# Order of GpSimd's and VectorE's work in a two-layer hypergraph block: the older group's power and the whole xb come first

## What is computed

```
H   = (adj != 0)
D   = 1 / sum_e H[c,e] w[e]          w = first row of adj
B   = 1 / sum_c H[c,e]
conv(x, W, b) = D * H (B * H^T (x W^T)) + b
h   = relu(conv(x, W1, b1))          256 -> 512
h   = layer_norm(h) * gamma + beta
y   = conv(h, W2, b2)                512 -> 256
out = layer_norm(x + (y + x))
```

## Time and profile before

| | |
|---|---|
| time of three executions | 327.19 us median, 326.97 to 327.41 |
| the profiled execution | 326.02 us, its span 324.1 us |
| granted TensorE clock over the span | 0.994 of full speed |
| busy: PE, DVE, ACT, POOL | 291.9, 228.6, 209.5, 143.0 us |
| make_h (L584) and add_pair (L650), 158.18 us, with POOL idle, in the turn shown | 0.42 and 0.68 us |
| one turn of the main loop in mid kernel | 18.98 us (normalise, L478, of two groups running: 132.19 and 151.17 us) |

### The profile page before, as it was taken

One profiled execution on the slowest core, in us unless ns is written; L12 is line 12 of the kernel. 1 busy time (PEld: TensorE's weight loads), 2 busy tenths in 40 slices (PEclk: granted clock), 3 DMA queues, 4 the chain that ended last, 5 costly groups with the idle time before them and its releaser, 6 DMA issues.

```text
span 324.1 us, 5911 instructions
## 1 busy us (share of the span) xinstructions
PE 291.9 (90%) x1866; PEld 251.0 (77%) x1866; DVE 228.6 (71%) x647; ACT 209.5 (65%) x621; POOL 143.0 (44%) x193
## 2 busy tenths in 40 slices
PE   6799889898989989898998989899898989999891
PEld 5689779696877969697795969779596877969690
DVE  2878597676849667685966768597676858668585
ACT  4478675777656577665657866566786656474713
POOL 2243524527064452716445171544617155553723
PEclk9999999999999999999999999999999999999997
DMA  7911400504123050412306042220403301010103
GB/s 237 270 34 50 115 0 14 166 2 141 40 73 107 5 174 3 134 46 59 119 3 179 2 124 54 53 97 3 147 0 115 98 1 67 0 65 2 65 3 129
DMA packets 33511, 24.28 MB, mean 75 GB/s; under 512 B 7932, under 2 KB 33224, under 8 KB 33480
## 3 DMA queue, kind: packets, MB, share of 16 engines
q1 hardware_dynamic: 33376, 23.86, 24.5%
q10 hardware_dynamic: 104, 0.04, 0.0%
HBM read 13.80 MB, written 8.39 MB: 68 GB/s over the span
## 4 chain that ended last, share of the span: by engine, by line
issue 50%; POOL 29%; PE 9%; DVE 8%; ACT 3%; DVEq 0%; POOLq 0%; ACTq 0%
POOL r_hi L858 11%; POOL rstd L842 6%; POOL rstd L865 5%; POOL xb_sb L850 4%; DVE g_sb L636 3%; PE bank_v L274 2%; DVE mv_sb L689 1%; PE bank_s L238 1%; PE bank_v L259 1%; PE bank_s L341 1%; POOL shift L873 1%; PE bank_g L291 1%; DVE var L693 1%; PE bank_g L284 1%; ACT r_sb L466 1%
## 5 line engine op out<-in xcount | busy, mean ns | idle before, releaser
L842 POOL TENSOR_TENSOR rstd<-stat,half_power 128x2 f32<-128x2 f32 x32 | 22.7, 711 | 130.0 <-DVE stat L626 130.0
L858 POOL TENSOR_SCALAR r_hi<-r_sb 128x512 fp32r<-128x512 f32 x64 | 53.0, 836 | 32.2 <-ACT r_sb L466 32.2
L284 PE MATMUL bank_g<-w_hi,r_hi 128*128 128x258 f32 x256 | 65.5, 288 | 0.0
L636 DVE SCALAR_TENSOR_TENSOR g_sb<-bank_g,rstd,c 128x256 f32<-128x256 f32 x64 | 28.1, 480 | 52.5 <-POOL rstd L842 52.5
L478 ACT ACTIVATE z_sb<-z_sb,shift,rstd 128x256 f32<-128x256 f32 x60 | 32.5, 590 | 49.6 <-POOL shift L873 49.6
L286 PE MATMUL bank_g<-w_lo,r_hi 128*128 128x256 f32 x256 | 63.8, 282 | 0.0
L274 PE MATMUL bank_v<-u_hi,w_hi 128*128 128x512 f32 x128 | 52.1, 407 | 10.8 <-ACT r_sb L466 10.2
L274 PE MATMUL bank_v<-u_hi,w_lo 128*128 128x512 f32 x128 | 50.8, 397 | 0.0
L274 PE MATMUL bank_v<-u_lo,w_hi 128*128 128x512 f32 x128 | 50.6, 395 | 0.0
L284 PEld LDWEIGHTS bank_g<-w_hi,r_hi 128*128 128x128 f32 x256 | 48.3, 189 | 1.4
L286 PEld LDWEIGHTS bank_g<-w_lo,r_hi 128*128 128x128 f32 x256 | 48.2, 188 | 1.2
(11 more groups left out here) (98 smaller groups left out, 476.4 us busy)
## 6 DMA issues: line engine op xcount, KB each, us to landing
x_sb<-in_x_dram SPq DMA_DIRECT2D x16, 512.0 KB, 3.9
out_dram<-z_sb SPq DMA_DIRECT2D x15, 512.0 KB, 3.2
adj_sb<-in_adj_dram SPq DMA_DIRECT2D x16, 256.0 KB, 3.7
w_raw<-in_L_gnn_W_dram SPq DMA_DIRECT2D x2, 512.0 KB, 4.9
out_dram<-z_sb SPq DMA_DIRECT2D x2, 256.0 KB, 2.6
turned_h<-h_sb SPq DMA_TRANSPOSE x13, 2.4
b_half<-in_L_gnn_b_dram SPq DMA_DIRECT2D x1, 128.0 KB, 8.1
edge_rows<-in_adj_dram ACTq DMA_DIRECT2D x1, 32.0 KB, 3.2
```

The lines of the kernel that those rows point to most:

```text
L284: pe.matmul(bank_g[:, n, 0:W2COLS], r_hi[:, i % 2, k, graph(n)], w2_hi[:, k], start=(k == 0), stop=False)
L636: ins = nc.vector.scalar_tensor_tensor(out=g_sb[:, n], in0=bank_g[:, n, 0:DOUT], scalar=rstd1[:, n:n + 1], in1=c2[:, :], op0=ALU.mult, op1 ...
L842: nc.gpsimd.tensor_tensor(rstd1[:, part], stat1[:, 3, part], half_power[:, part], ALU.pow).then_inc(rstd1_ready, 1)
L858: nc.gpsimd.tensor_scalar(r_hi[:, i % 2, k], r_sb[:, k], 1.0, 1.0, ALU.mult, ALU.mult).then_inc(r_hi_ready, 1)
```

## The change

On POOL the order of a turn becomes copy_w(i+3), add_b2(i+1) for the whole group, inverse_std2(i-1), inverse_std1(i,0), split_r(i+1,0), split_r(i+1,1), inverse_std1(i,1), split_r(i+1,2), split_r(i+1,3). `add_b2` is one instruction of 128x1024 instead of two of 128x512, and waits for all low parts of the group before (`r_lo_ready`), so that it starts when DVE has done `split_r(i,3)`, beside `split_u`. On DVE `make_var2(i-1)` and `make_h(i+4)` come ahead of `read_g(i,0)`: make_var2 before make_var1(i,0), make_h after it. The counts of `xb_ready` are halved where they are waited for.

```diff
@@ SyncE, load_x
-                    sp.wait_ge(xb_ready, (j - 2) * 2)
+                    sp.wait_ge(xb_ready, j - 2)
@@ PE, ahead of the last group's z
-            pe.wait_ge(xb_ready, G * 2)
+            pe.wait_ge(xb_ready, G)
@@ DVE, make_z
-                    dve.wait_ge(xb_ready, (i + 1) * 2)
+                    dve.wait_ge(xb_ready, i + 1)
@@ DVE, main loop
-                make_var1(i, 0)
-                read_g(i, 0)
                 if i:
                     make_var2(i - 1)
-                    if i + 4 < G:
-                        make_h(i + 4)
+                make_var1(i, 0)
+                if i and i + 4 < G:
+                    make_h(i + 4)
+                read_g(i, 0)
                 split_r(i + 1, 0)
                 make_var1(i, 1)
@@ POOL
-            def add_b2(i, half):
-                part, n = graphs(half), len(each(half))
+            def add_b2(i):
                 pool.wait_ge(x_in[i % 3], landed(i, 3))
-                if i >= 2 and half != 1:
+                if i >= 2:
                     pool.wait_ge(z_ready, (i - 1) * 2)
-                nc.gpsimd.tensor_tensor(xb_sb[:, i % 2, part], x_sb[:, i % 3, part],
-                                        b2_half[:, :].unsqueeze(1).to_broadcast([P, n, DOUT]),
-                                        ALU.add).then_inc(xb_ready, 1 if half is not None else 2)
+                if i:
+                    pool.wait_ge(r_lo_ready, i * KH)
+                nc.gpsimd.tensor_tensor(xb_sb[:, i % 2], x_sb[:, i % 3],
+                                        b2_half[:, :].unsqueeze(1).to_broadcast([P, PER, DOUT]),
+                                        ALU.add).then_inc(xb_ready, 1)
@@ POOL, main loop
-            add_b2(0, None)
+            add_b2(0)
 
             for i in range(LAST):
                 if i + 3 < G:
                     copy_w(i + 3)
-                inverse_std1(i, 0)
-                add_b2(i + 1, 0)
-                split_r(i + 1, 0)
+                add_b2(i + 1)
                 if i:
                     inverse_std2(i - 1)
+                inverse_std1(i, 0)
+                split_r(i + 1, 0)
                 split_r(i + 1, 1)
                 inverse_std1(i, 1)
-                add_b2(i + 1, 1)
                 split_r(i + 1, 2)
                 split_r(i + 1, 3)
```

## The result

The changed kernel takes 299.12 us (median of 4, 298.84 to 299.20) against 327.15 us: a ratio of 0.914, 95% interval 0.9125 to 0.9157. Beside the later experiments it took 299.2 us once more. The forecast was 303.4, in a range of 299.0 to 311.0: the measured time is inside, but only 0.12 us above the low end. The sum's 23.8 us compare with 27.2 us between the two profiled spans.

A forecast was written before the change was run, and what follows sets the result against it. PE, busy 291.9 of 324.1 us, bounds the kernel; its idle time comes from ACT's wait for POOL's late shift. 12 x 1.85 + 2.8 - 1.2 = 23.8 us gained gives a median of 303.4 us, range 299.0 to 311.0.

The forecast's parts named there:

- the low end: Fast bound of the time: 12 turns at 2.2 us plus 3 less 0.5 gives 298.3, taken as 299.0 us.
- The sum: Whole kernel: 12 turns x 1.85, plus 2 x 1.4, less 1.2 us, makes 23.8 us gained.
- What bounds, and the release of ACT: POOL's late shift holds ACT's normalise and ReLUs, delaying PE's make_v chunk 3 and make_y; at most 2.2 us a turn.
- The second half's chain: POOL and DVE from inverse_std1(i,1) to make_z: make_u starts 2.0 us sooner, DVE 0.3 behind PE's best.
- xb beside u_lo: Whole xb on POOL holds DVE's binv (L601) for 0.15 to 0.5 us; 0.15 taken, turn's gain rounded to 1.85.
- The first rival: POOL's split_r(i+1,3) gets the ports before DVE's add_pair: 1.35 us gained a turn, time 309.6 us; chance 0.24.
- The first turn: xb(1) right behind xb(0) holds DVE's two add_pair, u_lo and turn_q: 1.2 us lost, bounds 0 and 2.2.
- The last two turns: Same waits with less ACT work ahead: three quarters of a turn's gain, 1.4 us each, bounds 0.5 and 2.0.

The follow-up runs named there:

- The powers alone: Kernel before with the new order of powers on POOL and make_var2 on DVE, xb still in halves at its old places: 316.4 us, ratio 0.968.
- xb alone: Changed kernel's whole, early xb, with the powers and DVE's order as in the kernel before: 317.9 us, ratio 0.972.
- xb in halves: Changed kernel with xb as two half instructions at the new place: 299.27 us, ratio 0.915.
- half a pad: Changed kernel with one added 128x512 POOL instruction, like half of xb, ahead of xb in turns 1 to 13: 313.9 us, ratio 0.958.
- `make_s` first: Changed kernel with make_s(i+3) ahead of make_u(i+2) on PE: 294.81 us, ratio 0.901.
- The added wait: Changed kernel with xb of group 1 waiting on POOL until add_pairs of group 0 is done: 297.49 us, ratio 0.911.
- an explicit wait: Tested by removing xb's wait for DVE's low parts (`r_lo_ready`) from the changed kernel: 318.8 and 321.3 us, ratio 0.979.
- One program: Changed kernel with a second whole xb-like POOL instruction ahead of xb, turns 1 to 13: 303.65, 324.33, then 302.73, 303.58, 322.52 and 325.07 us.

## Why the prediction was right, and where its sizes were off

*What bounds, and the release of ACT: right.* The wait of L274 is gone, `make_y` took 1.89 us (forecast "about 1.9"). The powers alone and xb alone each give about a third of a turn's gain, so the two parts had to be worked out as one chain on POOL, as they were.

*The second half's chain: right.* I had `make_u` 2.0 us earlier with DVE 0.3 us behind PE's best. It is 2.01 us earlier in each turn; DVE waits 0.28 us for the first half of y at 145.04, and `make_s` in its place gave 0.35 us a turn.

*xb beside u_lo: mis-sized.* I took 0.15 us a turn for xb's hold on binv, 1.8 us in all. xb took 2.40 us, not 2.6 to 2.9 (the 2.88 of the earlier trace rows held a wait for DVE's r_lo ahead of it, as I read it now; that was not tried alone), and ended at 151.60 when binv came: 0.17 us, no hold. (With the 2.88 it would have ended 6.2 us after `make_u`'s start, not 6.25.) Nor would 0.15 have cost anything: in the run with xb in halves a hold of 0.34 us left its turn as long as before. One of 1.0 us cost 0.93 us in the run with half a pad. In the run with `make_s` first 0.5 us cost nothing, but there `make_s` gives cover that the changed kernel lacks, so what 0.5 us costs in the changed kernel no run shows. The rule of the shared ports, taken from the Trainium skill, page "SBUF — State Buffer", section "Who interferes with whom", spoke against the change only if something that matters waits behind xb. Nothing did, and one long xb was no worse than two short ones (299.2 and 299.27 us).

*The first rival: not taken.* DVE did get the ports first: add_pair (144.09) runs 0.68 us and r_hi behind it is held (0.84 at 144.40). r_lo (0.80 us at 143.37) was held as forecast. The rival's order, POOL first, is what happens in the run with half a pad, where add_pair takes 1.10 us and PE waits 0.92 us. DVE was ahead by 0.3 us here, where I had 0.15: the margin was real but small.

*The first turn: mechanism right, size off.* DVE's two add_pair and PE's wait behind them, with PE's later wait for the ReLU:

```profile
27.30 3.32 DVE L650 TENSOR_TENSOR pair_sb<-sq_sb 128x512 f32<-128x512 f32 x2
```

```profile
31.40 0.66 PE L301 MATMUL bank_g<-ident,q_sb 128*128 128x128 f32 x4 [1.31 <-DVE q_sb L657]
...
41.84 2.34 PE L308 MATMUL bank_v<-g_sb,at_sb 128*128 128x256 f32 x8 [1.24 <-ACT r_sb L466]
```

3.32 us instead of 1.26, and 1.31 us of idle PE at turn_q. But the wait at `make_y` fell from 2.4 to 1.24 us, since the half xb that stood ahead of r_hi in that turn is gone too. I had put down 1.2 us; the traces show 0.25 lost, or 0.56 without the earlier start of that execution. The added wait took back 1.7, more than was lost, because it keeps the gain of the missing half xb.

*The last two turns:* 1.3 and 1.6 us against 1.4 each, and 0.5 behind them that I had not counted. The three terms together (1.8, 0.95, 0.65) are the 3.4 us between the sum and the traces; 0.3 of the 0.95 is the earlier start. The median is 4.3 us below the forecast. The other 0.9 us is no part of the mechanism: I had added 1.2 us for a profiled execution below its median, and after the change that distance was 0.28 us. All these errors went the same way, and the time stayed in the range by only 0.12 us. I had worked out 298.3 for the low end and rounded it up to 299.0.

## What to carry to other kernels

When an engine that works in order waits for a small late result, everything urgent behind that wait is late in each turn: look for the wait whose releaser stands in a queue behind work that nobody needs yet. Work for GpSimd belongs beside operations of VectorE that it doesn't hold (here u_lo: 1.28 us for two, with xb running beside it), and such a place can be worth an explicit wait, here about 20 us; how much free time GpSimd has says nothing of what the work costs. Once no wait of the matrix engine is left in the waits view, compare a block's span with its undisturbed matmuls: here 0.28 us a turn hid there.

## What the runs showed that I had not expected

One program had two times in six executions, about 303 and 323 us, with nothing between. A tie of a few hundredths of a us between two engines, seen in every later turn of the traces of two low ones, is the likely cause; none of the high ones was traced. And added work of 1.3 us cost more (14.7 us in all) than added work of 2.4 us in its better runs (about 4).
